# A gated cross-attention layer on one core: the two score matmuls of each slot change places on TensorE

## The reference

```
q = Wq @ LN(x) + bq ; k = Wk @ ctx + bk ; v = Wv @ ctx + bv
dot  = mask * (q.T k / sqrt(32)) - (1 - mask) * 1e6
amap = softmax(dot, axis=-1) * mask
x = x + tanh(g_xattn) * (amap v)
x = x + tanh(g_ffn) * (fp8(LN(x) * s) / s) @ (fp8(W2 * s1) / s1)
```

## Time and profile before

| | us |
|---|---|
| three runs | 2498.09, 2502.59, 2505.27 (median 2502.59) |
| the profiled execution | 2498.55, its span 2496.9 |
| PE busy in the span | 2441.7 (98%) |
| DVE busy | 1960.7 (79%) |
| POOL busy | 1643.2 (66%) |
| ACT busy | 1387.1 (56%) |

### The profile page before, as it was taken

The page is one execution under the profiler, slowest core; times in us unless marked ns, Lnnn a source line. Parts: engine busy times, 40 slices in busy tenths (PEclk is TensorE's granted clock), DMA queues, the critical chain, the costliest instruction groups (busy, mean ns, idle before and its releaser), DMA issues.

```text
span 2496.9 us, 40504 instructions
## 1 busy us (share of the span) xinstructions
PE 2441.7 (98%) x13116; PEld 1382.0 (55%) x13177; DVE 1960.7 (79%) x3259; ACT 1387.1 (56%) x2606; POOL 1643.2 (66%) x1259
## 2 busy tenths in 40 slices
PE   7999999999999999999999999999999999999997
PEld 5888888875444444444444444444444444444442
DVE  6677776687788888888888888888888888888885
ACT  3333333315666666666666666666666666666664
POOL 2443333426777777777777777777777777777775
PEclk9999999999999999999999999999999999999999
DMA  6766666664444444444444444444444444444411
GB/s 245 262 243 237 234 235 235 227 188 100 94 102 98 102 101 102 97 94 95 94 93 100 92 92 92 92 92 101 92 93 95 99 101 102 98 101 97 104 45 56
DMA packets 241807, 313.48 MB, mean 126 GB/s; under 512 B 75000, under 2 KB 142648, under 8 KB 241624
## 3 DMA queue, kind: packets, MB, share of 16 engines
q1 hardware_dynamic: 230776, 275.56, 44.0%
q10 hardware_dynamic: 10848, 35.66, 4.0%
HBM read 199.83 MB, written 101.38 MB: 121 GB/s over the span
## 4 chain that ended last, share of the span: by engine, by line
PE 94%; DVE 1%; DMA 1%; issue 1%; POOL 1%; ACT 1%; SPq 0%; POOLq 0%; ACTq 0%; DVEq 0%
PE bank L863 22%; PE bank L893 20%; PE bank L848 20%; PE bank L878 19%; PE bank L904 9%; PE bank L940 4%; PE bank L933 1%; POOL pair_sum L398 1%; DMA q_st<-qx_scr 0%; DMA w_nat<-in_L_xattn_Wk_dram 0%; DMA v_scr<-stage 0%; ACT probs L715 0%; DVE x_raw L1043 0%; PE bank L802 0%; PE bank L924 0%
## 5 line engine op out<-in xcount | busy, mean ns | idle before, releaser
L398 POOL TENSOR_TENSOR pair_sum<-probs 128x512 f32<-128x512 f32 x1020 | 1279.2, 1286 | 399.0 <-ACT probs L715 399.0
L1143 DVE TENSOR_REDUCE part_max<-bank 128x1 f32<-128x512 f32 x2048 | 1276.6, 682 | 242.7 <-PE bank L878 229.2
L715 ACT ACTIVATE probs<-bank 128x512 f32<-128x512 f32 x2048 | 1067.4, 604 | 601.7 <-PE bank L863 578.7
L863 PE MATMUL bank<-q_st,k_st 100*128 100x512 f32 x2048 | 866.3, 425 | 6.0 <-ACT probs L715 6.0
L878 PE MATMUL bank<-k_st,q_st 98*128 98x512 f32 x2048 | 817.4, 399 | 8.3 <-DVE part_max L1143 6.5
L863 PEld LDWEIGHTS bank<-q_st,k_st 100*128 100x128 f32 x2048 | 387.4, 190 | 410.3 <-issue 211.2
L893 PE MATMUL bank<-probs,v_t 128*32 128x512 f32 x4096 | 545.6, 605 | 0.0
L878 PEld LDWEIGHTS bank<-k_st,q_st 98*128 98x128 f32 x2048 | 388.7, 190 | 129.2 <-DVE part_max L1143 15.8
L389 POOL TENSOR_TENSOR stage_lo<-stage,stage_hi 128x512 fp32r<-128x512 f32 x128 | 186.6, 1483 | 137.7 <-ACT stage_hi L661 136.2
L904 PE MATMUL bank<-pair_sum,ones 128*32 128x512 f32 x2040 | 265.5, 592 | 0.0
L661 ACT ACTIVATE stage_hi<-stage 128x512 fp32r<-128x512 f32 x128 | 80.2, 633 | 205.1 <-DVE stage L1007 142.9
(11 more groups left out here) (112 smaller groups left out, 2007.3 us busy)
## 6 DMA issues: line engine op xcount, KB each, us to landing
k_st<-k_scr SPq DMA_DIRECT2D x96, 512.0 KB
q_st<-q_scr SPq DMA_DIRECT2D x192, 256.0 KB
c_raw<-in_ctx_dram ACTq DMA_DIRECT2D x32, 512.0 KB, 7.0
k_scr<-stage_hi SPq DMA_DIRECT2D x64, 256.0 KB, 2.5
k_scr<-stage_lo SPq DMA_DIRECT2D x64, 256.0 KB, 2.7
v_scr<-stage SPq DMA_DIRECT2D x64, 256.0 KB, 2.9
q_scr<-stage_hi SPq DMA_DIRECT2D x64, 256.0 KB, 2.4
q_scr<-stage_lo SPq DMA_DIRECT2D x64, 256.0 KB, 2.7
```

Source lines behind the costliest of these rows:

```text
L398: nc.gpsimd.tensor_tensor(pair_sum[:, r % 2, h], probs[:, a, h], probs[:, a + 1, h], ALU.add).then_inc(pair_done, 1)
L715: nc.scalar.activation(probs[:, c % PR, h, :], s_bank_of(n, k)[:, :], ACT.Exp).then_inc(exp_done, 1)
L863: nc.tensor.matmul(s_bank_of(n, k)[:, :], k_st[p][0:KS, h, j * P:(j + 1) * P], q_st[p][0:KS, th, h, :], start=True, stop=True).then_inc(sc ...
L1143: nc.vector.tensor_reduce(part_max[:, th, sh, at:at + 1], x_bank_of(n, "tile", k)[:, :], AX, ALU.max).then_inc(max_done, 2)
```

## The change

In TensorE's list for a slot, the matmul of the max pass is now issued first and the exponential's score tile second. Nothing else is changed: no other engine's list, no bank, no semaphore count.

```diff
                     def slot(n, p, k):
                         m, odd, i = maxima_at(n, k)
+                        if real(m):
+                            scores_for_max(n, k, m, (p + odd) % 2, i)
                         if real(n):
                             scores(n, p, k)
-                        if real(m):
-                            scores_for_max(n, k, m, (p + odd) % 2, i)
                         if k % 4 == 3:
                             if k >= 7 and real(n):
                                 times_v(n, p, (k - 7) // 4)
```

## The result

The changed kernel takes 2533.43 us in the median of four runs (2530.55 to 2534.52), the kernel before 2503.93 (2498.09 to 2506.45): 1.0119 times as long, 95% interval 1.0102 to 1.0136, or 29.5 us slower. The direction was forecast, 2517.0 us was not, and the time lies above the range (2506 to 2527). The forecast mechanism is there with its size, 14 us. As much again comes from two places that I had counted at nothing, where VectorE and GpSimd meet.

A forecast was written before the change was run, and what follows sets the result against it. TensorE, 98% busy, was taken as the bound. Ordinary groups and late loads counted 0; groups behind feed-forward halves cost 60 x 0.24 = 14.4 us, so 2502.6 + 14.4 = 2517.0 us, range 2506 to 2527.

The forecast's parts named there:

- forecast mechanism: Behind feed-forward halves, the fourth x still waits for its reduction and one more s stands behind it: 0.24 us, 60 times, 14.4 us.
- TensorE bounds the stage: Attention stage: TensorE is busy 98% of the span, so only distances between its starts count, including delays the idle column hides.
- Behind a feed-forward half: Slots 32 to 35 and 48 to 51: VectorE's reductions follow the feed-forward matmuls' end, so x's load comes no earlier; 14.4 us.
- Rival 1: Behind feed-forward halves: the load runs ahead and only the matmul waits; 0.13 us each, 8 us, 2510 in all; chance 0.08.
- rival 2: Behind feed-forward halves: the reductions move forward with x, so the price is 0 and the time 2502.6 us; chance 0.13.
- Late loads in front of s: Ordinary groups: the last x's load, 0.08 us late, now precedes an s; taken as 0, at most 34 us; chance 0.09.
- Ordinary groups: Groups not behind a feed-forward half: x one place (0.23 us) earlier, s one later, waits keep their slack; 2.07 us to V.

## Why the prediction was wrong

- *TensorE bounds the stage, and distances between starts are what to read*: right. Every loss was found there; the idle column of the matmuls grew by 2.2 us in all.
- *Behind a feed-forward half the releaser hangs on the matmuls' end and not on x; price 0.24 us x 60 = 14.4 us*: right. 0.24 in both halves, 13.9 us in the trace of the change, 14.0 us by itself. The places are 58 and not 60: tile i of a quad stands in slot i + 19 of the period before (`maxima_at`), so x runs 45 slots ahead of its use and not 19, and the last period has none behind slot 18. That is worth 0.5 us. Rival 1 (the load runs ahead) asked for V at 2.36 and 2.42 us, and rival 2 for the old 2.23 and 2.29; the trace has 2.46 and 2.53.
- *Late loads in front of s, taken at 0 with 34 us as the upper bound*: right at 0.
- *"Ordinary groups": "Both streams keep their distances", "Cost: 0"*: this step failed, and with it the sum. The x stream kept its distances and so did the s stream, but they move against each other, by 0.47 us, and each drives an engine: x drives VectorE, s by way of the exponentials GpSimd. I asked only what the two streams wait for on semaphores. VectorE's small operations of slots 19 and 55 also wait for the GpSimd addition in progress, without a semaphore, and that wait depends on the distance. In the 14 traces, 1096 of these operations (L1152, L1157, L1159, L1171) from 600 us on took over 0.05 us more than their shortest, and every one ended within 0.05 us of the end of a GpSimd instruction. It cost 10.6 and 6.4 us in the changed kernel's trace, 18.5 us by itself in a run. Take GpSimd away and both go (2.07 and 2.01 us); shift GpSimd alone and one comes without the change (2.44 us).
- The sign of it was in view. In the kernel before, L1171 took 0.68 us for 16 columns in the period of the earlier trace rows where its shortest was 0.23, and L1152 at 0.17 us started 0.06 us short of the addition's end. I read a row for the reductions and one for the addition of each half, and none for what stands between the reductions of a group and those of the next.
- The rule was there too. The Trainium skill ("SBUF — State Buffer", SBUF: two separate sides) says that VectorE and GpSimd share one pair of SBUF ports under an exclusive lock held for the whole instruction, and that VectorE needs it in a two-port mode or, against a GpSimd instruction that reads SBUF, with two SBUF inputs. The traces agree: the elementwise maximum (0.56 us), the scaling of one tensor (0.36 for L1157, up to 1.21 for L1171) and the two-input multiply (up to 1.42) end within 0.05 us of an addition's end, and the reciprocal (0.25 at most) and the reduction (0.19 at most) never wait. Which mode the scaling ran in no trace shows. My first version of the theory, two inputs only, was narrower than the rule, and the scaling showed it.

What stays open: the first stage ends between 568 and 572 us and the first period of the attention stage takes 56 to 60 us in the different traces, also between kernels that do not differ there. That is some us of noise in single comparisons, and its cause was not looked for. Why the inverse of slot 23 starts later in every fourth period was not looked for either.

## What to carry to other kernels

Where two streams on the bounding engine drive two other engines, a change of their order shifts these engines against each other. List everything that couples them, not the semaphores alone: for VectorE and GpSimd look for short VectorE operations whose longest or median duration is well above their shortest, and see whether they end with a GpSimd instruction. Where such an operation sits between two runs of work that free buffers for the bounding engine, its worst case (here one addition of 1.28 us) belongs in the range of any change that moves either side. And a wait shows first in what stands behind it: count the instructions of the bounding engine behind a fixed release, before and after.

## What the runs showed of the hardware that I had not expected

- A VectorE operation on 16 columns took from 0.23 to 1.42 us depending on where in a GpSimd addition it started, and ended 0.03 to 0.04 us after the addition's recorded end. Started about 0.1 us ahead of that end, it took either 0.24 us or 1.40, to the end of the next addition. With one input a scaling waits as an operation with two does (0.86 us in the median both ways); a reciprocal and a reduction from SBUF do not (0.25 and 0.18 us).
- When the first operation of a chain is freed of the wait, the next one of the waiting kind inherits it (0.36 instead of 0.17 us), so only part is gained: slots 20 to 23 went from 2.44 to 2.24 us and not to 2.07.
- A GpSimd fill of 0.5 us in a span in which GpSimd is 66% busy cost the kernel 26.8 us, more than the 16.7 us that its 32 executions took: it paid in TensorE's time, twice in each period.
- A weight load that is up to 0.13 us late costs TensorE nothing (the load of x19 in the kernel before, followed by V after the usual 0.33 us); beyond that, the traces' three cases cost about what they were late by, less some 0.12: 0.17 us late cost 0.06 (x35 before), 0.24 cost 0.13 (x51 before), 0.51 cost 0.37 (x23 after).
- In the run whose TensorE waits 1.4 us once in most periods (x35 and x51 behind V), its granted clock fell from 1.0 to 0.50 in 11 places, at 0.43 us from matmul to matmul instead of 0.23; in the same stage of the kernel before it never fell.
